# Middle layers of a four-layer decoder: the second norm's high part is made by VectorE instead of ScalarE

## The reference, cut to what matters

```python
sa = _mha(x, x, x, tgt_mask, ...)                    # 16 heads of 16 features
x = _ln(x + sa, ln1_g, ln1_b)
ca = _mha(x, enc_output, enc_output, memory_mask, ...)
x = _ln(x + ca, ln2_g, ln2_b)                        # the second norm
ff = relu(x @ ff_w1 + ff_b1) @ ff_w2 + ff_b2         # 256 -> 1024 -> 256
x = _ln(x + ff, ln3_g, ln3_b)
```

## Time and profile before

| what | value |
|---|---|
| median of the three runs | 3352.99 us |
| the profiled execution's own time | 3355.26 us |
| its span | 3353.6 us |
| mean granted TensorE clock | 0.959 |
| TensorE (PE) busy | 3019.1 us, 90% |
| VectorE (DVE) busy | 2043.1 us, 61% |
| ScalarE (ACT) busy | 1894.9 us, 57% |
| GpSimd (POOL) busy | 1487.5 us, 44% |

### The profile page before, as it was taken

One profiled execution on the slowest core, in us unless ns is written; L12 is line 12 of the kernel. 1 busy time (PEld: TensorE's weight loads), 2 busy tenths in 40 slices (PEclk: granted clock), 3 DMA queues, 4 the chain that ended last, 5 costly groups with the idle time before them and its releaser, 6 DMA issues. The chain is left out here.

```text
span 3353.6 us, 82485 instructions
## 1 busy us (share of the span) xinstructions
PE 3019.1 (90%) x28656; PEld 2682.5 (80%) x28656; DVE 2043.1 (61%) x4340; ACT 1894.9 (57%) x7796; POOL 1487.5 (44%) x1874
## 2 busy tenths in 40 slices
PE   8999999689999999637999999999999999847886
PEld 6999998479999999636888888888888888746665
DVE  3445454244444444336777787788778877726775
ACT  3444444134444444326777777777777777616664
POOL 1233422103444544611555555555555555543545
PEclk9999999899999999868999999999999999978998
DMA  3112221311111110032222222333111111123331
GB/s 131 58 57 68 80 76 38 132 48 39 45 53 53 53 46 20 35 129 78 86 74 70 67 69 73 95 93 123 56 58 59 61 61 57 33 69 97 96 100 40
DMA packets 218390, 232.87 MB, mean 69 GB/s; under 512 B 41952, under 2 KB 183264, under 8 KB 215904
## 3 DMA queue, kind: packets, MB, share of 16 engines
q1 hardware_dynamic: 218208, 230.49, 21.6%
HBM read 148.57 MB, written 65.01 MB: 64 GB/s over the span
## 5 line engine op out<-in xcount | busy, mean ns | idle before, releaser
L1757 ACT ACTIVATE middle_stage<-middle_psum,middle_neg_max 128x128 f32<-128x128 f32 x2048 | 726.1, 391 | 330.4 <-DVE middle_neg_max L1737 330.2
L1757 ACT ACTIVATION_READ_ACCUMULATOR middle_stage<-middle_psum,middle_neg_max 128x1 f32 x2048 | 471.8, 230 | 0.0
L1737 DVE TENSOR_REDUCE middle_neg_max<-middle_psum 128x4 f32<-128x512 f32 x512 | 337.3, 680 | 51.2 <-PE middle_psum L1700 49.1
L1711 PE MATMUL middle_psum<-middle_eye,middle_stage 128*128 128x128 f32 x2048 | 321.5, 280 | 18.4 <-DVE middle_stage L1743 8.3
L1711 PEld LDWEIGHTS middle_psum<-middle_eye,middle_stage 128*128 128x128 f32 x2048 | 231.9, 142 | 71.8 <-issue 46.4
L1666 POOL TENSOR_TENSOR middle_attended_lo<-middle_mix,middle_attended_hi 128x256 fp32r<-128x256 f32 x128 | 94.9, 741 | 436.4 <-DVE middle_attended_hi L1749 436.4
L1757 ACT ACTIVATE fourth_stage<-fourth_psum,fourth_neg_max 128x128 f32<-128x128 f32 x512 | 182.9, 400 | 93.5 <-DVE fourth_neg_max L1737 93.4
L536 POOL TENSOR_TENSOR cross_ff_hidden_lo<-cross_ff_relu,cross_ff_hidden_hi 128x256 fp32r<-128x256 f32 x128 | 100.9, 789 | 279.7 <-DVE cross_ff_hidden_hi L531 279.7
L97 PE MATMUL middle_psum<-middle_n_yt_hi,middle_w_lo 128*128 128x256 f32 x640 | 194.1, 303 | 13.7 <-ACT middle_n_y L1874 12.1
L1967 POOL TENSOR_TENSOR middle_ff_hidden_lo<-middle_ff_relu,middle_ff_hidden_hi 128x256 fp32r<-128x256 f32 x256 | 183.5, 737 | 48.8 <-DVE middle_ff_hidden_hi L1961 48.8
L1743 DVE COPY middle_stage<-middle_psum 128x512 f32<-128x512 f32 x256 | 175.2, 684 | 16.8 <-PE middle_psum L1711 16.5
(11 more groups left out here) (351 smaller groups left out, 10910.4 us busy)
## 6 DMA issues: line engine op xcount, KB each, us to landing
middle_stage<-middle_a_k SPq DMA_DIRECT2D x1024, 16.0 KB, 1.8
middle_xt_hi<-x_hi SPq DMA_DIRECT2D x32, 256.0 KB, 2.7
middle_xt_lo<-x_lo SPq DMA_DIRECT2D x32, 256.0 KB, 3.0
middle_mask_flags<-flags SPq DMA_DIRECT2D x128, 64.0 KB, 1.9
middle_ct_hi<-context_hi SPq DMA_DIRECT2D x32, 256.0 KB, 2.9
middle_ct_lo<-context_lo SPq DMA_DIRECT2D x32, 256.0 KB, 3.1
middle_x_rows<-x_rows SPq DMA_DIRECT2D x32, 256.0 KB, 2.7
x_rows<-middle_n_z SPq DMA_DIRECT2D x32, 256.0 KB, 2.2
```

The costliest lines, as they stand in the source:

```text
L1711: ins = pe.transpose(banks.psum[:, TURN_BANK, x * SEQ:(x + 1) * SEQ], self.sh.p_wide[:, 4 * b + t, x, :], self.sh.eye[:])
L1737: dve.tensor_reduce(self.sh.neg_max[:, 4 * b + t, :], psum[:, SCORE_BANKS[t], :].rearrange("p (x k) -> p x k", x=4), AX_X, ALU.max, negate ...
L1757: ins = act.activation(self.sh.p_wide[:, 4 * b + t, x, :], psum[:, SCORE_BANKS[t], x * SEQ:(x + 1) * SEQ], ACT.Exp, bias=self.sh.neg_max[: ...
```

## The change

The second norm's high part leaves ScalarE's stream and enters VectorE's stream, directly ahead of the low part. Its destination, source and semaphores stay the same: it waits for the eviction and signals `hi_ready`.

```diff
@@ scalar, section x1
                 exp(x1_next, 1)
                 if ok(-2):
                     norm2.act(act, Back(r, 2), psum)
-                    norm2.act_hi(act, Back(r, 2))
                 spread(x1)
                 exp(x1_next, 2)
@@ vector, section x1
                 turned(x1[1], 2)
                 if ok(-2):
+                    norm2.dve_hi(dve, Back(r, 2))
                     norm2.dve_lo(dve, Back(r, 2))
                 norm(x1[0])
```

## The result

The changed kernel takes 3336.68 us (median of 5 runs, 3326.49 to 3338.62) against 3350.19 us before (median of 5, 3346.86 to 3356.8). The ratio of the runs is 0.9945, 95% interval 0.9933 to 0.9958. On a second occasion it was 0.9931, 0.9910 to 0.9952 (3335.47 against 3356.54 us). The forecast, 3332.3 to 3352.99, is a ratio of 0.9938. The direction, the place and the size were right; some details inside were not.

What follows compares the result with a forecast made beforehand. TensorE was taken as the bound, its gap at y0's scores set by ScalarE's chain; 30 rounds x 0.69 us = 20.7 us off the median 3352.99 gave 3332.3 us, range 3328 to 3339 (80 in 100).

Steps and rivals of the forecast that it cites:

- The bound and the wait: TensorE, 97% busy, bounds; at y0's start its scores wait 0.76 us (L1), 0.67 us (L2) for ScalarE's last x1 exponential.
- 0.69 us a round from ScalarE: In x1, eviction to spread on ScalarE falls from 1.59 to 0.90 us, so all behind it comes 0.69 us sooner.
- Count and sum: 30 rounds x 0.69 us = 20.7 us gained; fill rounds and drain counted as nothing.
- The floor: TensorE's own work lets y0's scores start 0.75 us (L2) or 0.84 us (L1) sooner; ScalarE stays later by 0.06 and 0.15.
- The second rival: The low part in x1 paces TensorE, so only its 0.20 us a round is gained: 6 us, 3347.0 us; 7 in 100.
- VectorE's cover: In x1 VectorE's 0.75 us idle ahead of the low part covers the 0.43 us cast; low part 0.20 us sooner.
- GpSimd: GpSimd colliding with VectorE's cast and low part in x1, 1.08 us each, would cost 33 us, 3386 us; 3 in 100.
- The third rival: A transfer or VectorE instruction now just in time elsewhere in the round takes back the 0.69 us: 3353 us; 7 in 100.

Runs made afterwards that it cites:

- kernel a: The changed kernel, with ScalarE copying the second norm's 512 columns into an unused tile where its cast stood; ratio to the kernel before 0.9996.
- Kernel c: The changed kernel, with the third norm's high part (section x0) also moved from ScalarE to VectorE; ratio to the kernel before 0.9984.
- Kernel p: The changed kernel, with two GpSimd additions of 512 columns released beside VectorE's new cast in section x1; ratio to the kernel before 0.9969.
- e: The changed kernel, with TensorE's output product of hidden unit 3 put ahead of hidden product 4 in section y1; ratio to the kernel before 0.9954.
- i: The changed kernel, with VectorE's first maximum of section y1 put between the two halves of the norm's moments; ratio to the kernel before 0.9966.
- j: The changed kernel, with VectorE's first maximum in sections x1 and y1 put between the halves of the norm's moments; ratio to the kernel before 1.0004.
- h: The kernel before the change, with TensorE's first turning of section y0 put ahead of the scores, ScalarE's cast kept; ratio to the kernel before 0.9973.
- b: The changed kernel, with VectorE casting the second norm's 512 columns twice in section x1, first into an unused tile; ratio to the kernel before 0.9953.
- f: The changed kernel, with TensorE's first turning of section y0 put ahead of the scores; ratio to the kernel before 0.9920.

## Why the prediction was right, step by step

- *The bound and the wait.* Right. TensorE's idle time at the start of y0 was sold, and kernel a, which restores ScalarE's chain and nothing else, brings it back.
- *0.69 us a round from ScalarE.* Nearly. Eviction to spread is 0.90 us as in the earlier trace rows, but from the eviction's start to the end of the last read the chain is 2479.03 - 2474.94 = 4.09 instead of 4.75 us, 0.66 less: the same exponentials keep their step of 0.34 us, and the last one shows 0.45 instead of 0.41 us. Section x1 became 0.67 and 0.66 us shorter. The round of L1 gained 0.64 us. L2 gained 0.70 to 0.80 us; about 0.1 us of that lies in section y1, which the prediction didn't have and which kernel a gains too, without ScalarE's part.
- *Count and sum.* The stretch gained 22.7 and 19.7 us in its two profiles, where 20.7 was forecast for the whole. The measured medians lie 13.5 and 21.1 us apart; the ratio 0.9945 is 18 us. That the sum fits so closely is in part luck: the 0.1 us a round of y1 in L2 was not in it, and the draining rounds alone move the stretch by 2 us from one profile to the next.
- *The floor.* ScalarE is still the later one in both layers, as forecast, but what is left of the gap is 0.23 and 0.14 us, not 0.07 and nothing. The forecast had assumed that the feed-forward product gains nothing from the earlier low part. It does: in L2 its second matmul, the first one that reads the low part, came 2481.94 - 2481.72 = 0.22 us after the first before and 2477.54 - 2477.43 = 0.11 us after it now, and its last matmul starts 2478.67 - 2474.94 = 3.73 us after the eviction's start instead of 2483.11 - 2479.25 = 3.86 (3.74 instead of 3.87 in L1). Kernel a, which shares the early low part alone, has the same 0.11 us. The row that the views above lack, from the kernel before:

```profile
2481.94 0.28 PE L97 MATMUL middle_psum<-middle_n_yt_lo,middle_w_hi 128*128 128x256 f32 x1
```

  This does not count as long as ScalarE ends last. The second rival had this much truth in it.
- *VectorE's cover.* Right: the cast starts 0.03 us after the eviction's end and takes 0.43 us, the low part is ready 2477.16 - 2475.97 = 1.19 us after it (1.18 forecast), and the reciprocal finds VectorE free, with no marked wait. Kernel c is the counter-proof, 0.47 us a round where such cover is missing.
- *GpSimd.* Right to be given little: it is idle for 5.87 us around the cast in the changed kernel. Kernel p shows that the collision exists and what it costs. What the prediction calls a multiply-add of GpSimd in the earlier trace rows is a plain addition (L1853).

The third rival, the gap that comes back elsewhere, did not come true for the change; it did for e, and in another form for i, j and h.

## What to carry to other kernels

An instruction moved between engines is worth its length only where the engine that loses it is the last to release the bound engine, and costs nothing only where the engine that gets it stands idle at that very point: look for both in the timeline of that place, not in the busy shares. The same cast, moved the same way, gave 0.66 us a round in one section and took 0.47 us in another. Filling the idle time of the bound engine with its own later work wins only up to the next thing which that work waits for. Before an instruction is moved forward in a queue, read on to the next instruction that others wait for: what is pushed behind may hold that one.

## What the runs showed of the hardware

- The same cast of 128x512 float32 to fp32r takes 0.62 us on ScalarE and 0.43 us on VectorE.
- A GpSimd addition that began first held VectorE's cast up by 0.55 us (0.98 instead of 0.43).
- TensorE's turning into a PSUM bank starts 0.13 us after the VectorE copy that reads the bank has ended (2658.08 against 2657.27 + 0.68 = 2657.95 in kernel h; the same 0.13 us in the medians of b, f and p).
- ScalarE's activations without a semaphore between them overlap: spread behind eviction starts 0.13 us before the eviction ends (2475.84 against 2475.97), while a cast that waits for the eviction starts 0.03 us after it. That is why the removal gave more than the 0.53 us from the cast's start to the spread's.
